# The mask of a graph layer, turned by the DMA instead of by TensorE

## The reference

```
agg = matmul(adj, layernorm(x))
x   = x + relu(matmul(agg, W.T) + b)
```

## Time and profile before

| | us |
|---|---|
| median of 3 runs (lowest, highest) | 1818.52 (1814.2, 1821.43) |
| profiled execution | 1819.35 |
| its span | 1817.8 |

### The profile page before, as it was taken

One profiled execution on the slowest core, in us unless ns is written; L12 is line 12 of the kernel. 1 busy time (PEld: TensorE's weight loads), 2 busy tenths in 40 slices (PEclk: granted clock), 3 DMA queues, 4 the chain that ended last, 5 costly groups with the idle time before them and its releaser, 6 DMA issues. The chain is left out here.

```text
span 1817.8 us, 36040 instructions
## 1 busy us (share of the span) xinstructions
PE 1551.0 (85%) x9584; PEld 1291.5 (71%) x9584; DVE 1150.7 (63%) x3860; ACT 638.9 (35%) x1349; POOL 698.9 (38%) x1336
## 2 busy tenths in 40 slices
PE   5899999999999925999999339999618999999994
PEld 4888888888888724887888326555307888888894
DVE  5467777777777776566655346666685666666652
ACT  2333333333333301322223243222205565555562
POOL 0122322232222213776667204443414555455551
PEclk9899999999999966999999769999858999999997
DMA  6324344333334353333333424555341222222223
GB/s 94 111 109 150 136 145 151 132 130 130 130 132 146 98 196 114 51 49 49 52 49 50 98 94 153 195 205 195 110 189 30 41 35 38 38 35 36 40 37 91
DMA packets 85363, 184.70 MB, mean 102 GB/s; under 512 B 19790, under 2 KB 62540, under 8 KB 81292
## 3 DMA queue, kind: packets, MB, share of 16 engines
q1 hardware_dynamic: 57386, 128.02, 21.6%
q0 software_dynamic: 22656, 31.07, 11.2%
q10 hardware_dynamic: 5280, 25.17, 3.5%
HBM read 132.66 MB, written 54.99 MB: 103 GB/s over the span
## 5 line engine op out<-in xcount | busy, mean ns | idle before, releaser
L1112 PE MATMUL bank<-ffn_w_in_parts,ffn_x_t 128*128 128x512 f32 x1416 | 361.1, 403 | 1.7 <-DVE ffn_w_in_parts L1251 1.7
L1136 PE MATMUL bank<-ffn_w_out_parts,ffn_hidden_t 128*128 128x256 f32 x2124 | 285.0, 288 | 19.5 <-DVE ffn_hidden_t L1241 19.5
L1112 PEld LDWEIGHTS bank<-ffn_w_in_parts,ffn_x_t 128*128 128x128 f32 x1416 | 258.9, 190 | 55.9 <-DVE ffn_w_in_parts L1251 5.0
L1136 PEld LDWEIGHTS bank<-ffn_w_out_parts,ffn_hidden_t 128*128 128x128 f32 x2124 | 263.2, 192 | 25.1 <-issue 16.2
L624 PE MATMUL bank<-h_t,attn_h_tile 128*128 128x512 f32 (+1 forms) x1092 | 248.8, 383 | 3.9 <-POOL attn_h_tile L493 3.9
L659 PE MATMUL bank<-support,attn_probs_t 128*128 128x512 f32 x650 | 246.7, 413 | 5.1 <-DVE attn_probs_t L533 4.7
L624 PEld LDWEIGHTS bank<-h_t,attn_h_tile 128*128 128x128 f32 x1092 | 197.0, 189 | 46.1 <-issue 4.1
L521 ACT CAST attn_probs_t<-bank 128x512 fp32r<-128x512 f32 (+1 forms) x182 | 98.7, 557 | 357.5 <-PE bank L633 357.5
L1076 POOL DMA_INDIRECT x<-ffn_y,ffn_dst x118 | 196.5, 1665 | 53.6 <-issue 53.6
L1178 ACT ACTIVATE ffn_silu_or_gelu<-bank,w_b_in 128x128 f32<-128x128 f32 x472 | 134.6, 368 | 155.9 <-PE bank L1123 155.9
L661 PE MATMUL bank<-support,attn_probs_t 128*128 128x256 f32 x676 | 185.0, 280 | 0.0
(11 more groups left out here) (248 smaller groups left out, 2388.5 us busy)
## 6 DMA issues: line engine op xcount, KB each, us to landing
adj_tile<-in_adj SPq DMA_DIRECT2D x25, 1663.5 KB, 7.6
mask<-attn_mask ACTq DMA_DIRECT2D x26, 832.0 KB, 3.4
nbr_mask<-mask SPq DMA_DIRECT2D x26, 832.0 KB, 5.1
w_w_in<-in_w SPq DMA_DIRECT2D x16, 512.0 KB, 10.5
w_w_in<-in_w_t SPq DMA_DIRECT2D x16, 512.0 KB, 4.2
w_w_out<-in_w SPq DMA_DIRECT2D x1, 4096.0 KB, 20.5
x<-attn_x_out SPq DMA_DIRECT2D x26, 128.0 KB, 1.7
xn<-attn_x_normed SPq DMA_DIRECT2D x26, 128.0 KB, 2.5
```

The source lines that it names most:

```text
L1112: ins = pe.matmul(bank[2 + 2 * slot + b][:, :], XT[:, slot, xp, k, :], WIP[:, wp, k, b * CH:(b + 1) * CH], start=n == 0 and k == 0, stop=n ...
L1136: ins = pe.matmul(bank[7][:, 0:D], HTT[:, hp, k, :], WOP[:, wp, k, :], start=n == 0 and k == 0, stop=n == 2 and k == KH - 1)
```

## The change

The load of a mask becomes a transposing DMA, so that block j of tile t arrives with its 128 columns on the partitions. PE's flips, its identity in bf16 and the two PSUM banks for them go. `AT` holds two whole tiles instead of two groups. ACT converts the 14 blocks of groups 0 and 1 of a tile in one instruction (`front`), DVE the 12 of groups 2 and 3 in another (`back`), both from SBUF. Each does it one tile ahead: in step t for tile t+1, after it has waited for that tile's DMA and until tile t-1 has been multiplied. PE waits for `front` ahead of group 0 and for `back` ahead of group 2. SP asks for mask t once tile t-2 has been converted; the rest of its step stays as it was.

```diff
@@ -1347,9 +1347,9 @@
     assert G % 2 == 0
     with ExitStack() as ctx:
         s = Stage(nc, ctx, "nbr")
-        NEG = s.sb("mask", [P, 2, NP], BF16)
-        ID, IDF = s.sb("identity", [P, P], BF16), s.sb("identity_f32", [P, P])
-        AT = s.sb("adj_t", [P, 2, 8 * P], F16)
+        MT = s.sb("mask_t", [P, 2, T, P], BF16)
+        IDF = s.sb("identity_f32", [P, P])
+        AT = s.sb("adj_t", [P, 2, T, P], F16)
         WT = s.sb("w_t", [P, KD, D])
         BB = s.sb("bias", [P, D])
         XB, XO = s.sb("x", [P, 2, D]), s.sb("x_out", [P, 2, D])
@@ -1360,12 +1360,12 @@
         mask_in = [s.sem(f"mask_loaded{i}") for i in range(2)]
         x_loaded = [s.sem(f"x_loaded{i}") for i in range(2)]
         x_stored = [s.sem(f"x_stored{i}") for i in range(2)]
-        flipped, at_ready, used = s.sem("mask_transposed"), s.sem("adj_t_ready"), s.sem("group_multiplied")
-        at_odd = s.sem("adj_t_odd_ready")
+        front_ready, back_ready, used = s.sem("adj_t_front_ready"), s.sem("adj_t_back_ready"), s.sem("group_multiplied")
         hi_ready, ag_ready, ag_flipped, agt_ready = s.sem("sum_hi_ready"), s.sem("sum_ready"), s.sem("sum_transposed"), s.sem("sum_t_ready")
         out_done, pre_ready, x_ready = s.sem("product_ready"), s.sem("pre_ready"), s.sem("x_ready")
         gate = Gate(s, XO, gate_w, None, LG, a["xn"])
-        bf = [bank[i][:, :].bitcast(BF16) for i in range(2)]
+
+        FRONT = GS[2][0]
         with nc.Block() as block:
             @block.sync
             def _(sp):
@@ -1375,8 +1375,9 @@
 
                 def step(t, uses, slot, first, last):
                     if not first:
-                        sp.wait_ge(flipped, (t - 1) * G)
-                    sp.dma_start(NEG[:, slot, :], a["mask"][t, :, :]).then_inc(mask_in[slot], 16)
+                        sp.wait_ge(front_ready, t - 1)
+                        sp.wait_ge(back_ready, t - 1)
+                    sp.dma_start_transpose(MT[:, slot, :, :], a["mask"][t, :, :]).then_inc(mask_in[slot], 16)
                     if not known(t) or t >= 3:
                         gate.store(sp, t - 3, 1 - slot)
                     if not first:
@@ -1396,32 +1397,23 @@
 
             @block.gpsimd
             def _(pool):
-                for n, i in enumerate((ID, IDF)):
-                    pool.memset(i[:], 0.0).then_inc(consts, 1)
-                    pool.wait_ge(consts, 2 * n + 1)
-                    pool.affine_select(out=i[:], in_=i[:], compare_op=ALU.not_equal, fill=1.0, base=0,
-                                       pattern=[[-1, P]], channel_multiplier=1).then_inc(consts, 1)
+                pool.memset(IDF[:], 0.0).then_inc(consts, 1)
+                pool.wait_ge(consts, 1)
+                pool.affine_select(out=IDF[:], in_=IDF[:], compare_op=ALU.not_equal, fill=1.0, base=0,
+                                   pattern=[[-1, P]], channel_multiplier=1).then_inc(consts, 1)
                 gate.constants(pool)
                 tiles(pool, T, lambda t, uses, slot, first, last: gate.norm(pool, t, uses, slot))
 
             @block.tensor
             def _(pe):
-                def flip(t, uses, slot, g, first):
+                def multiply(t, slot, g):
                     g0, gn = GS[g]
                     if g == 0:
-                        pe.wait_ge(mask_in[slot], (uses + 1) * 16)
-                    if not (first and slot == 0 and g < 2):
-
-                        pe.wait_ge(at_ready if g % 2 == 0 else at_odd, t * (G // 2) + g // 2)
+                        pe.wait_ge(front_ready, t + 1)
+                    if g0 == FRONT:
+                        pe.wait_ge(back_ready, t + 1)
                     for j in range(gn):
-                        ins = pe.transpose(bf[g % 2][:, j * P:(j + 1) * P], NEG[:, slot, (g0 + j) * P:(g0 + j + 1) * P], ID[:])
-                    ins.then_inc(flipped, 1)
-
-                def multiply(t, slot, g):
-                    g0, gn = GS[g]
-                    pe.wait_ge(at_ready if g % 2 == 0 else at_odd, t * (G // 2) + g // 2 + 1)
-                    for j in range(gn):
-                        ins = pe.matmul(bank[2 + slot][:, :], AT[:, g % 2, j * P:(j + 1) * P],
+                        ins = pe.matmul(bank[2 + slot][:, :], AT[:, slot, g0 + j, :],
                                         XH[:, g0 + j, :, :].rearrange("p a d -> p (a d)"), start=g0 + j == 0, stop=g0 + j == T - 1)
                     ins.then_inc(used, 1)
 
@@ -1444,10 +1436,6 @@
                     if not first:
                         pe.wait_ge(ag_ready, t - 1)
                     for g in range(G):
-                        if g + 1 < G:
-                            flip(t, uses, slot, g + 1, first)
-                        elif not last:
-                            flip(t + 1, uses + slot, 1 - slot, 0, first and slot == 0)
                         multiply(t, slot, g)
                         if g == 1 and not very_first:
                             finish(t - 1, 1 - slot, first)
@@ -1456,8 +1444,7 @@
                     if last:
                         finish(t, slot, False)
                         project_out(t, slot)
-                pe.wait_ge(consts, 4)
-                flip(0, 0, 0, 0, True)
+                pe.wait_ge(consts, 2)
                 pe.wait_ge(w_loaded, 32)
                 tiles(pe, T, step)
 
@@ -1467,13 +1454,11 @@
                 act.dma_start(BB[:], a["b"].partition_broadcast(P)).then_inc(w_loaded, 16)
                 gate.load(act)
 
-                def even(t, slot, g, first):
-                    act.wait_ge(flipped, t * G + g + 1)
-                    if not (first and slot == 0 and g < 2):
-                        act.wait_ge(used, t * G + g - 1)
-                    w = GS[g][1] * P
-
-                    act.activation(AT[:, 0, 0:w], bf[0][:, 0:w], ACT.Copy, bias=1.0, scale=1.0 / BIG).then_inc(at_ready, 1)
+                def front(t, uses, slot):
+                    act.wait_ge(mask_in[slot], (uses + 1) * 16)
+                    if not known(t) or t >= 2:
+                        act.wait_ge(used, (t - 1) * G)
+                    act.activation(AT[:, slot, 0:FRONT, :], MT[:, slot, 0:FRONT, :], ACT.Copy, bias=1.0, scale=1.0 / BIG).then_inc(front_ready, 1)
 
                 def tail(t, slot, first):
                     act.wait_ge(used, (t + 1) * G)
@@ -1488,25 +1473,25 @@
                     act.copy(AGT[:, slot, :, :], bank[4 + slot][:, 0:D].rearrange("p (k n) -> p k n", k=KD)).then_inc(agt_ready, 1)
 
                 def step(t, uses, slot, first, last):
-                    for g in range(0, G, 2):
-                        even(t, slot, g, first)
-                        if g == 0 and not (first and slot == 0):
-                            tail(t - 1, 1 - slot, first)
+                    if not (first and slot == 0):
+                        tail(t - 1, 1 - slot, first)
+                    if not last:
+                        front(t + 1, uses + slot, 1 - slot)
                     if not (first and slot == 0):
                         flip_out(t - 1, 1 - slot, first)
                     if last:
                         tail(t, slot, False)
                         flip_out(t, slot, False)
+                front(0, 0, 0)
                 tiles(act, T, step)
 
             @block.vector
             def _(dve):
-                def odd(t, slot, g, first):
-                    if not (first and slot == 0 and g < 2):
-                        dve.wait_ge(used, t * G + g - 1)
-                    dve.wait_ge(flipped, t * G + g + 1)
-                    w = GS[g][1] * P
-                    dve.tensor_scalar(AT[:, 1, 0:w], bf[1][:, 0:w], 1.0 / BIG, 1.0, ALU.mult, ALU.add).then_inc(at_odd, 1)
+                def back(t, uses, slot):
+                    if not known(t) or t >= 2:
+                        dve.wait_ge(used, (t - 1) * G)
+                    dve.wait_ge(mask_in[slot], (uses + 1) * 16)
+                    dve.tensor_scalar(AT[:, slot, FRONT:T, :], MT[:, slot, FRONT:T, :], 1.0 / BIG, 1.0, ALU.mult, ALU.add).then_inc(back_ready, 1)
 
                 def add(t, slot, first):
                     dve.wait_ge(hi_ready, t + 1)
@@ -1535,10 +1520,10 @@
                     very_first = first and slot == 0
                     if not very_first:
                         add(t - 1, 1 - slot, first)
-                    odd(t, slot, 1, first)
+                    if not last:
+                        back(t + 1, uses + slot, 1 - slot)
                     if not known(t) or t >= 3:
                         logits(t - 3, 1 - slot)
-                    odd(t, slot, 3, first)
                     if not very_first:
                         finish(t - 1, uses - (1 - slot), 1 - slot, first)
                     if last:
@@ -1547,6 +1532,7 @@
                         finish(t, uses, slot, False)
                         logits(t - 1, 1 - slot)
                         logits(t, slot)
+                back(0, 0, 0)
                 tiles(dve, T, step, head=4)
```

## The result

| | before | after |
|---|---|---|
| median, us (lowest to highest) | 1819.13 (1814.2 to 1821.43) | 1942.16 (1941.11 to 1948.16) |
| span of the profiled execution, us | 1817.8 | 1940.8 |
| first mask's issue to the last product's end, us | 233.8 | 355.4 |
| from there to the end of the span, us | 518.1 | 519.6 |

The changed kernel takes 1.0686 times as long (95% interval 1.0662 to 1.071). The forecast was 1930 with a range from 1885 to 2010, and slower with a chance of 0.93. Of the 123 us lost, 121.6 lie in the neighbour loop; what follows it is 1.5 us longer than before. Masks, tiles and turns are numbered from 0.

What follows compares the result with a forecast made beforehand. PE was taken to bound the neighbour loop at about 8.15 us a tile. The sum was 1819.35 + 73 (loop closed within one tile) + 34.5 (slower transposing transfer) + 3.5 (clock) = 1930 us, range 1885 to 2010.

Steps and rivals of the forecast that it cites:

- The bound and what goes: Neighbour loop: PE bounds at about 8.15 us a tile; flips cost 1.46 us of it, 47 us in all with mask waits.
- The rival in which the loop does not close: Mask there before DVE reaches its conversion, PE the bound at 6.7 us a tile: 1772 us; chance 0.04 faster.
- The loop within one tile: Next mask is asked for only after the last has landed and DVE's queued work is done: +73 us.
- the sum: Turn terms added: 10.7 us without a weight piece, 12.7 with one, plus T; over 22 turns, last product 73 us later.
- 3.5 for the clock: Price of bursts at half clock, given as 4 to 6 us and taken as 3.5 us.
- T: Extra landing time of a transposing mask transfer over a plain one: 1.5 us each, 34.5 us in all.
- the clock's 0.2 a turn: Allowance in each turn for project_out taking 2.02 us at half clock and just about ending with DVE.
- The signs named in advance: PE busy half the stage; DVE and ACT waiting 5 to 8 us a tile; masks every 12 or 14 us.
- The terms of the turn: Mask issue to issue: landing 4.5 or 5.3 us, release 0.1, back 0.9, logits 3.3, finish 0.98, SP 0.9 or 2.1.
- the longer branch: After landing, DVE's 4.3 us was to cover the 3.4 us on ACT and PE, by 0.9 us.
- Mask 3 was to be issued at 1089.5: Start of the loop: mask 3, issued at 1092.24 before, comes at about 1089.5 without the 46 flips ahead of it.
- The clock: PE's bursts begin at half clock in the loop; 0.2 us a turn and 2 us in the last burst, taken as 3.5.

Runs made afterwards that it cites:

- e11: The kernel before the change (flips on TensorE, plain DMA) with SP asking for mask t+1 in step t, ahead of the store: 1810.7 us.
- e12: e10 with the gate's weights loaded by ACT as eight loads of 128 KB over its first three steps: 1773.3 us.
- e1: The changed kernel with each mask brought by a plain DMA, row by row, all queues in the same order: 1902.6 us.
- e2: The changed kernel with SP asking for mask t+1 in step t, ahead of the store of tile t-2: 1805.7 us.
- e3: The changed kernel with DVE's conversion moved behind finish and ACT's behind flip_out, SP's order kept: 1836.4 us.
- e4: The changed kernel with the mask brought by a plain DMA in 3328 pieces of 256 bytes per tile: 1944.5 us.
- e6: The changed kernel with 20 idle products of 512 columns added on TensorE ahead of project_out of every tile: 1944.6 us.
- e7: The changed kernel with DVE's conversion alone moved behind logits and finish: 1941.5 us.
- e8: The changed kernel with ACT's conversion alone moved behind flip_out: 1927.4 us.
- e5: The changed kernel with ACT loading the gate's weights only once the second mask has landed: 1934.3 us.
- e9: e2 with ACT loading the gate's weights only once the second mask has landed: 1807.8 us.
- e10: e9 with the 16 weight pieces issued at the end of ACT's steps, not on SP's queue: 1787.1 us.

## Why the prediction was right

**The bound and what goes.** PE was the bound at 8.15 us a tile, as e11 shows by the waits being gone: every turn 8.15. That 1.46 us of it were flips also holds, nearly: from 8.15 to 6.78 in e12 it is 1.37. The rival in which the loop does not close was priced at 1772 and said to be open only if the mask is there in time; e12, which makes it so, takes 1773.3. It did more than the rival assumed, though: it moved two other loads as well.

**The loop within one tile.** Right, and the main step. e1 isolates it: with plain transfers the loop lasts 311.1 us against 233.8, 77 us more, where the sum said 73 and 3.5 for the clock. Its turns, 12.92 and 10.46, were put at 12.7 and 10.7. e2 and e3 open it from two ends. From mask 3 to mask 25 the sum gave 300 us with T (305 with the clock's 0.2 a turn); the trace has 298.1 (1104.41 to 1402.49). The signs named in advance came too: DVE and ACT waited 6.9 and 7.4 us a tile for the mask's DMA, a mask was issued every 11.2 and 14.3 us, and SP's longest wait was still that for x_out. PE was busy for 64% of the stage, not half.

**The terms of the turn.** A turn with a piece has three parts. From issue to DVE's conversion it was put at 6.9 us (5.3, 0.1 and T) and took 6.96. From there to x_out's end it was put at 5.2 and took 5.07. From there to the next mask it was put at 2.1 and took 2.24. Inside the second part two errors nearly cancel. The conversion on DVE took 0.56, not 0.9: from SBUF it was cheaper than the slope from PSUM. On ACT it took 1.70, as said (1.67). DVE was to be the longer branch, by 0.9 us or nothing at half clock; in fact ACT's and PE's branch ends 0.46 us after DVE's, since DVE was faster than put.

**T.** Put at 1.5 us. Against e1 the turns differ by 1.35 with a piece and 0.73 without; 16 and 6 of them make 26 us, where 33 was put. The Trainium skill's sentence that transposing DMAs are as fast as regular ones (Advanced Engine Details and Errata, X-Bar Transpose (TRN2)) holds beside a plain DMA of the same pieces (e4), not beside one of whole rows: 5.6 us against 4.6 to land.

**The start, which the sum lacked.** Mask 3 was to be issued at 1089.5 and was at 1104.41. The first product waited 24.1 us from the first issue instead of 9. No step of the prediction asked what the first transfer meets; it meets the gate's weights, which landed in 11 us beside plain masks and in 21.2 beside transposing ones (12.7 to 18.2 in e2, e3, e6, e7 and e8). The profile before showed both loads at that place. By the medians of e5 and the changed kernel the start is worth 8 us, by the profiled executions up to 15. That is as large as the 12 by which the forecast was short, and a T put some 7 us too high gives part of it back: that the total came within 12 us is in part luck, that the loop did is not.

**The clock.** Right that bursts begin at half clock (0.80 granted on average, project_out in 2.07 us). Its price was put too low: 0.46 us in a turn with a piece, put at 0.2, some 7 us in 16 such turns where the sum had 3.5 in all. DVE's cheaper conversion (0.34 us a turn) gives about as much back.

## What to carry to other kernels

When work is moved from an engine into a DMA, ask what now waits for that DMA, what is queued behind that wait, and whether the next request for the same kind of transfer is behind the outcome of that work on the issuing queue. A prefetch that is written one tile ahead is none if its issue stands behind a store that needs the tile before it. Moving one issue up by one step was here worth 136 us, and with the other loads taken out of its way as well the change that had cost 7% gave 2.5%.

## What was not expected of the hardware

A transposing DMA of 832 KB holds SP for 3.4 to 3.8 us with no other load in flight and for 4.1 to 5.7 behind a weight piece (the changed kernel; up to 6.4 in e9), a plain one of the same pieces for 0.4. While another queue's 1 MB broadcast is in flight beside it, it holds SP for 7.2 to 15.4 us, and the first mask lands after 14.6 (e7) to 22.3 us (the changed kernel). A plain one in the same pieces landed after 7.8 beside the same broadcast (e4). With the broadcast behind it, in e10, the first lands after 8.7 us and the third, which meets it, after 15.5; with the same bytes as eight loads of 128 KB over three steps (e12) the third lands after 8.8. DVE's conversion of bf16 from SBUF took 0.56 us for 1536 columns, as long as it had taken from PSUM for 768.
